# Output projection of the second attention: one fp32 product over 12 chunks, or three fp32r products key head by key head

## What is computed

```python
def _L1_xattn_ref(latents, context, Wq, Wk, Wv, Wo):
    H, KV, HD = (16, 4, 96)
    G = H // KV
    hidden = jnp.concatenate([context, latents], axis=1)
    q = (latents @ Wq.T).reshape(b, q_len, H, HD)
    k = (hidden @ Wk.T).reshape(b, s_len, KV, HD)
    v = (hidden @ Wv.T).reshape(b, s_len, KV, HD)
    ...
    scores = jnp.einsum('bkgqd,bksd->bkgqs', q, k) * scale
    attn = jax.nn.softmax(scores.astype(jnp.float32), axis=-1).astype(q.dtype)
    out = jnp.einsum('bkgqs,bksd->bkgqd', attn, v)
    return out.transpose(...).reshape(b, q_len, H * HD) @ Wo.T
...
x = x + jnp.tanh(g_xattn[1]) * _L1_xattn_ref(_layernorm(x), ctx_4096, ...)
```

## Time and profile before

| | us |
|---|---|
| median of 3 runs | 1620.5 (1618.6 to 1621.03) |
| the profiled execution, its time | 1619.05 |
| the profiled execution, first to last instruction (span) | 1617.3 |
| PE busy in it | 1572.8 (97%) |
| second attention, four pairs | 896.6 to 1257.5 |

### The profile page before, as it was taken

The page is one execution under the profiler, slowest core; times in us unless marked ns, Lnnn a source line. Parts: engine busy times, 40 slices in busy tenths (PEclk is TensorE's granted clock), DMA queues, the critical chain, the costliest instruction groups (busy, mean ns, idle before and its releaser), DMA issues.

```text
span 1617.3 us, 25912 instructions
## 1 busy us (share of the span) xinstructions
PE 1572.8 (97%) x8958; PEld 1264.1 (78%) x8958; DVE 981.2 (61%) x2633; ACT 742.1 (46%) x2151; POOL 399.3 (25%) x278
## 2 busy tenths in 40 slices
PE   8999999999999999999989999999999999899997
PEld 7888888888888888888875877868696788666556
DVE  6762663626636356363676774848576767756677
ACT  5442443424434244343433462735355332288873
POOL 3131320313203132032204300000001343376651
PEclk9999999999999999999999999999999999999999
DMA  5111111101111011110224000000001613000001
GB/s 179 54 43 34 59 45 41 42 29 55 42 52 42 29 55 42 52 43 30 79 79 195 14 1 14 0 13 0 0 1 41 223 52 107 14 14 14 1 1 53
DMA packets 34436, 76.22 MB, mean 47 GB/s; under 512 B 5569, under 2 KB 18497, under 8 KB 32193
## 3 DMA queue, kind: packets, MB, share of 16 engines
q1 hardware_dynamic: 34368, 75.36, 14.1%
HBM read 73.25 MB, written 2.10 MB: 47 GB/s over the span
## 4 chain that ended last, share of the span: by engine, by line
PE 78%; DVE 10%; ACT 5%; issue 3%; DVEq 2%; POOL 1%; DMA 1%; POOLq 0%; SPq 0%; ACTq 0%
PE banks L1183 11%; PE banks L1128 10%; PE banks L1101 9%; PE banks L1109 9%; PE banks L1333 9%; PE banks L1437 5%; PE banks L1239 4%; PE banks L1222 3%; PE banks L1409 3%; ACT p L978 2%; PE banks L1229 2%; PE banks L1540 2%; PE banks L1563 1%; PE banks L1357 1%; PE banks L1547 1%
## 5 line engine op out<-in xcount | busy, mean ns | idle before, releaser
L1183 PE MATMUL banks<-w_o,atT 128*128 128x512 f32 x720 | 180.2, 396 | 0.0
L527 POOL TENSOR_TENSOR w_q<-w_raw_q,w_q 128x1792 fp32r<-128x1792 f32 x15 | 61.1, 4070 | 479.6 <-ACT w_q L733 479.6
L1101 PE MATMUL banks<-cT,w_k 128*128 128x512 f32 x720 | 178.0, 396 | 0.0
L1128 PE MATMUL banks<-w_v,cT 128*128 128x512 f32 x768 | 176.6, 390 | 0.0
L1128 PEld LDWEIGHTS banks<-w_v,cT 128*128 128x128 f32 x768 | 143.9, 188 | 29.9
L1109 PE MATMUL banks<-xT,w_q 128*128 128x512 f32 x672 | 163.8, 394 | 0.7 <-ACT kT L723 0.7
L1874 DVE TENSOR_TENSOR sA<-banks,pbias 128x512 f32<-128x512 f32 x64 | 44.1, 690 | 186.5 <-PE banks L1222 185.8
L1183 PEld LDWEIGHTS banks<-w_o,atT 128*128 128x128 f32 x720 | 131.9, 188 | 25.7
L1101 PEld LDWEIGHTS banks<-cT,w_k 128*128 128x128 f32 x720 | 131.9, 188 | 25.6
L1109 PEld LDWEIGHTS banks<-xT,w_q 128*128 128x128 f32 x672 | 123.7, 188 | 26.1 <-ACT kT L723 1.1
L792 ACT ACTIVATE sA<-sA,nmA 128x128 f32<-128x128 f32 x256 | 99.5, 393 | 56.9 <-DVE nmA L1879 56.6
(11 more groups left out here) (280 smaller groups left out, 3273.7 us busy)
## 6 DMA issues: line engine op xcount, KB each, us to landing
w_raw_v<-in_w0v SPq DMA_DIRECT2D x8, 1024.0 KB, 4.8
w_raw_q<-in_w0q SPq DMA_DIRECT2D x16, 512.0 KB, 3.3
w_raw_k<-in_w0k SPq DMA_DIRECT2D x15, 512.0 KB, 3.5
w_raw_o<-in_w0o SPq DMA_DIRECT2D x15, 512.0 KB, 3.3
cTp<-in_ctxT SPq DMA_DIRECT2D x12, 512.0 KB, 4.0
wq_raw<-in_wq SPq DMA_DIRECT2D x1, 3072.0 KB, 10.4
wo<-in_wo SPq DMA_DIRECT2D x1, 3072.0 KB, 20.1
x_res<-in_x SPq DMA_DIRECT2D x4, 512.0 KB, 11.3
```

What stands on the lines that cost most here:

```text
L527: pool.tensor_tensor(w_part[slot][1][:], w_raw[slot][:], w_part[slot][0][:].bitcast(F32), ALU.subtract).then_inc(S(f"w{slot}_lo"), 1)
L1101: mm = pe.matmul(dst, wk_[l][:, c, h * P:(h + 1) * P], cT[r][:, c, half * HT:(half + 1) * HT], start=c == 0 and n == 0, stop=c == DC - 1 a ...
L1128: mm = pe.matmul(dst, cT[l][:, c, b * P:(b + 1) * P], wv_[r][:, c, :], start=n == 0, stop=n == 3 * DC - 1)
L1183: mm = pe.matmul(dst, atT[l][:, h, t], w[r][:, h, :], start=n == 0, stop=n == 5)
```

## The change

`at1` is now three tiles of one key head: `at1_raw` in fp32, written by ACT alone, and two fp32r parts, which DVE makes by a cast and a subtraction (both from SBUF to SBUF). The weight comes in quarters, one for each key head and pair (16 loads of 768 KB where there was one of 3 MB), into two slots used in turn; ACT rounds a quarter in three pieces of 128x512 (`out_high`) and POOL subtracts in three (`out_rest`). `project(kv, b)` is 9 fp32r matmuls, run one key head later, and DVE adds each result to x (`add_out`, eight additions for a pair where there were two). Bank 6 + b now alternates between queries and projection, which `added` and the order of the queries guard. The next pair's rows are normalised before the loop over key heads and turned inside the last one, in banks 6 and 7; in the last pair they are turned between the last two projections. The waits for `at1` ahead of the scores become waits for ACT's copy (`x1_ah`).

```diff
@@ -271,9 +268,18 @@
...
-        wo1 = sb(ctx_1, "wo1", [P, NCH * KV1, D])
+
+        wo1, wo1_raw = [], []
+        for k in range(2):
+            high_1 = sb(ctx_1, f"wo1_0_{k}", [P, NCH, D], F32R)
+            ctx_x = ExitStack()
+            wo1_raw.append(sb(ctx_x, f"wo1_raw_{k}", [P, NCH, D]))
+            ctx_x.close()
+            wo1.append([high_1, sb(ctx_1, f"wo1_1_{k}", [P, NCH, D], F32R)])
...
+        at1_raw = sb(ctx_1, "at1_raw", [P, NCH, PT2])
+        at1 = [sb(ctx_1, f"at1_{l}", [P, NCH, PT2], F32R) for l in range(2)]
...
@@ -459,14 +465,30 @@
...
-            sp.dma_start(wo1[:], A["wo1"]).then_inc(S("wo1_ld"), 16)
...
+                sp.dma_start(wo1_raw[kv % 2][:], A["wo1"][:, NCH * kv:NCH * (kv + 1), :]).then_inc(S("wo1_ld"), 16)
...
+            def next_out_weights(i, kvs):
+                for kv in range(kvs):
+                    sp.wait_ge(S("x1_out"), 8 * i + 2 * kv + 2)
+                    out_weights(KV1 * i + kv + 2, (kv + 2) % KV1)
...
@@ -609,8 +631,16 @@
...
+            def out_rest(i, kv):
+                for c in range(NCH):
+                    pool.wait_ge(S("w1_hi"), KV1 + NCH * (KV1 * i + kv) + c + 1)
+                    pool.tensor_tensor(wo1[kv % 2][1][:, c, :], wo1_raw[kv % 2][:, c, :],
+                                       wo1[kv % 2][0][:, c, :].bitcast(F32), ALU.subtract).then_inc(S("w1_lo"), 1)
...
+                for kv in range(KV1):
+                    out_rest(i, kv)
...
@@ -909,31 +939,54 @@
...
+                def out_high(kv, c0, c1):
+                    if c0 == 0:
+                        act.wait_ge(S("wo1_ld"), 16 * (KV1 * i + kv + 1))
+                    for c in range(c0, c1):
+                        act.activation(wo1[kv % 2][0][:, c, :], wo1_raw[kv % 2][:, c, :], ACT.Copy)\
+                           .then_inc(S("w1_hi"), 1)
...
-                def attended(kv, b):
-                    act.wait_ge(S("x1_pv"), 8 * i + 2 * kv + b + 1)
+                out_high(0, 0, NCH)
+
+                def attended(kv, b, heads=True, rest=True):
...
+                    if heads:
+                        act.wait_ge(S("x1_pv"), 8 * i + 2 * kv + b + 1)
+                        act.activation(at1_raw[0:HD1, :, t], src[0:HD1, 0:NCH], ACT.Copy)
+                    if rest:
...
+                            e = act.activation(at1_raw[HD1:P, c, t], src[c * BLK:(c + 1) * BLK, G1 - 1], ACT.Copy)
+                        e.then_inc(S("x1_ah"), 1)
 
                 for kv in range(KV1):
+                    more = kv + 1 < KV1
+                    if kv > 0:
+                        out_high(kv, 0, 1)
                     probs(kv, 0)
+                    if kv > 0 and more:
+                        out_high(kv, 1, NCH)
                     probs(kv, 1)
-                    for b in range(2):
-                        probsT(kv, b)
-                        if kv + 1 < KV1:
-                            queries(kv + 1, 2 * b, min(2 * b + 2, NCH))
-                        attended(kv, b)
+                    probsT(kv, 0)
+                    if more:
+                        queries(kv + 1, 0, 2)
+                    else:
+                        out_high(kv, 1, NCH)
+                    attended(kv, 0, rest=False)
+                    probsT(kv, 1)
+                    attended(kv, 0, heads=False)
+                    if more:
+                        queries(kv + 1, 2, NCH)
+                    elif not last:
+                        store_xnT(L1X, i + 1, (0, 1), (6, 7))
+                    attended(kv, 1)
                 if not last:
                     context_high(i + 1)
                 else:
                     act.wait_ge(S("ffn_ld"), 128)
                     high(f1p[0], ffn["f1"]["base"][:], "wf")
-                store_next(L1X, i, last)
+                    store_next(L1X, i, last)
...
@@ -1405,6 +1458,8 @@
...
+                        if h == 0 and kv > 0:
+                            pe.wait_ge(S("x1_ah"), 8 * i + 2 * kv + b - 1)
...
@@ -1432,43 +1487,62 @@
...
+                def project(kv, b):
+                    pe.wait_ge(S("x1_at"), 8 * i + 2 * kv + b + 1)
+                    pe.wait_ge(S("w1_lo"), KV1 + NCH * (KV1 * i + kv + 1))
+                    if kv + 1 == KV1:
+                        if last:
+                            pe.wait_ge(S("x1_added"), 6 * i + 2 * kv + b - 1)
+                        else:
+                            wait_parts(L1X, i + 1, b)
+                    for c in range(NCH):
+                        for n, (l, r) in enumerate(PASSES):
+                            mm = pe.matmul(bank(6 + b), at1[l][:, c, b * P:(b + 1) * P], wo1[kv % 2][r][:, c, :],
+                                           start=c == 0 and n == 0, stop=c == NCH - 1 and n == len(PASSES) - 1)
+                    mm.then_inc(S("x1_out"), 1)
+
+                def added(kv, b):
+                    pe.wait_ge(S("x1_added"), 6 * i + 2 * kv + b + 1)
 
                 for kv in range(KV1):
+                    more = kv + 1 < KV1
                     for b in range(2):
                         if kv == 0:
                             pe.wait_ge(S("v1_ready"), 4 * i + 3 + b)
-                        else:
-                            pe.wait_ge(S(f"x1_at{b}"), 4 * i + kv)
                         scores(kv, b)
-                    more = kv + 1 < KV1
-                    if more:
-                        pe.wait_ge(S("wq1_lo"), kv + 2)
+                        if 0 < kv and more:
+                            project(kv - 1, b)
+                    if kv == 0:
+                        pe.wait_ge(S("w1_lo"), kv + 2)
                         queries(kv + 1, 0, 2)
                         queries(kv + 1, 2, NCH, 0, 1)
-                    else:
-                        pe.wait_ge(S("wo1_ld"), 16)
-                        project(0, 0, 2 * NCH - 1)
+                    if not more:
+                        project(kv - 1, 0)
                     for b in range(2):
                         turn(kv, b)
-                        if more:
+                        if kv == 0:
                             queries(kv + 1, 2, NCH, b + 1, 2 * b + 2)
-                        else:
-                            project(0, 2 * (NCH + b) - 1, 2 * (NCH + b) + 1)
+                        elif more:
+                            if b == 0:
+                                pe.wait_ge(S("w1_lo"), kv + 2)
+                                added(kv - 1, 0)
+                                queries(kv + 1, 0, 1)
+                                queries(kv + 1, 1, 2, 0, 2)
+                            else:
+                                queries(kv + 1, 1, 2, 2, DC)
+                                added(kv - 1, 1)
+                                queries(kv + 1, 2, NCH)
+                        elif b == 0:
+                            project(kv - 1, 1)
+                        elif not last:
+                            for j in range(2):
+                                added(kv - 1, j)
+                                turn_half(L1X, i + 1, j, 6 + j)
                         attend(kv, b)
-                project(0, 2 * NCH + 3, NCH * (KV1 - 1))
-                pe.wait_ge(S("x1_at0"), 4 * i + 4)
-                project(0, NCH * (KV1 - 1), NCH * KV1)
-                project(1, 0, 2 * NCH - 1)
-                turn_next(L1X, i, last)
-                project(1, 2 * NCH - 1, NCH * (KV1 - 1))
-                pe.wait_ge(S("x1_at1"), 4 * i + 4)
-                project(1, NCH * (KV1 - 1), NCH * KV1)
+                project(KV1 - 1, 0)
+                if last:
+                    turn_next(L1X, i, last)
+                project(KV1 - 1, 1)
...
@@ -2107,32 +2181,58 @@
...
+                def attended(kv, b):
+                    t = slice(b * P, (b + 1) * P)
+                    dve.wait_ge(S("x1_ah"), 8 * i + 2 * kv + b + 1)
+                    dve.tensor_copy(at1[0][:, :, t], at1_raw[:, :, t])
+                    dve.drain()
+                    dve.tensor_tensor(at1[1][:, :, t], at1_raw[:, :, t], at1[0][:, :, t].bitcast(F32),
+                                      ALU.subtract).then_inc(S("x1_at"), 1)
...
+                def add_out(kv, b):
+                    dve.wait_ge(S("x1_out"), 8 * i + 2 * kv + b + 1)
...
+                                             in1=x_res[:, 2 * i + b, :], op0=ALU.mult, op1=ALU.add)\
+                       .then_inc(S("res" if kv + 1 == KV1 else "x1_added"), 1)
+
+                next_apply(L1X, i)
                 for kv in range(KV1):
+                    more = kv + 1 < KV1
                     row_max(kv, 0)
-                    row_max(kv, 1)
-                    norm(kv, 0)
-                    norm(kv, 1)
+                    if kv > 0:
+                        attended(kv - 1, 1)
+                    if kv == 0:
+                        row_max(kv, 1)
+                        norm(kv, 0)
+                        norm(kv, 1)
+                    elif more:
+                        add_out(kv - 1, 0)
+                        norm(kv, 0)
```

(31 more changed lines are left out.)

53 lines of the change are left out of this document (22 added, 31 removed).

## The result

| | before | after |
|---|---|---|
| median, us | 1620.23 (4 runs, 1618.6 to 1621.03) | **1649.22** (4 runs, 1644.92 to 1650.57) |
| ratio | | 1.018, 95% interval 1.0165 to 1.0194 |
| span of the profiled execution | 1617.3 | 1647.3 |

The page's line of busy time answers to the earlier trace rows. PE's busy time is only 3.2 us less, since the length of a matmul in it is modelled and grows with a lower clock or a late neighbour; what a matmul costs is read from the spacing of starts. PE's share falls from 97% to 95% because the span is longer.

The account below looks back on a forecast made before the run. PE, busy 97%, bounds the kernel. A pair: +14.0 middle heads, −8.7 last head, −0.2 first, so +5.1; four pairs 20.4 plus end 2.9 give +23.3 on 1619.05, 1642.4; median 1.45 above, stated as 1643, range 1624 to 1652.

Parts of the forecast that it names:

- case A: The forecast itself: all the costed waits appear, 1636 to 1652 us; chance 0.58.
- below 3.8: Sign of being wrong: PE's waits in a second-attention pair grow by less than 3.8 us.
- Projection, −15.4: 72 fp32r matmuls a pair at 0.233 replace 24 fp32 chunks at 0.859: 3.8 us less a pair, 15.4 in all.
- Middle heads, 20.2: Key heads 1 and 2 take 20.2 us instead of 13.2: 4.2 of projection, 2.8 of waits; +14.0 a pair.
- The hold: POOL's weight subtractions hold DVE's scaling of p in middle heads; first turn waits from 7.7 to 8.5 us.
- case B: POOL's pieces miss the scaling of p, about 2 us less a head: 1627 us; chance 0.24.
- Last key head, 20.0: Each pair's last head, with two projections and waits of 2.0 and 1.3, takes 20.0 us, not 28.7: −8.7.
- First head, −0.2: First key head and before: a 0.5 us wait goes, normalising moved to DVE gives 0.35 back; −0.2 a pair.
- Stage end, +2.9: Once, after the last pair: PE waits 2.7 us for POOL's f1base split, plus 0.2 more in this pair.
- Costed at nothing: SP's 16 weight loads of 768 KB arrive in time, so no ACT rounding waits; zero cost.
- C: Projections fill PE under the score-to-turn chain, waits stay as before, only matmuls change: 1605 us; chance 0.07.
- Rival E: POOL holds more than the scaling, the casts and subtractions too: over 1652 us; chance 0.06.

Follow-up runs that it names:

- end_fp32r: Kernel before, own order, each fp32 projection matmul replaced by three fp32r ones on rounded operands, low parts left out: 1604.2 us.
- q_early: Changed kernel, with only TensorE finishing chunk 1 of the next queries ahead of the middle heads' second turn: 1626.9 us.
- late_pieces: Changed kernel, with the rounding of weight chunks 1 and 2 of the middle heads moved behind the first pT copies: 1632.6 us.
- small_pieces: Changed kernel, with POOL's weight subtractions cut to 8 of 512 columns and the third pass reading rounded weights: 1630.8 us.
- best_a: late_q_early plus f1_wait, with both third-head projections ahead of the last head's first turn and the next rows' split earlier: 1607.5 us.
- f1_wait: Changed kernel, with TensorE's wait for POOL's split of f1base put behind the 16 f1ra matmuls of its first pair: 1645.9 us.
- fp32_by_head: Changed kernel's head-by-head order with the projection in fp32 on raw weights and rows, no weight rounding or POOL split: 1643.1 us.
- late_q_early: late_pieces, with TensorE also finishing chunk 1 of the next queries ahead of the second turn: 1615.9 us.

## Why the prediction was right, and where it was off

The forecast was 1643, the likeliest case A, range 1624 to 1652; measured 1649.2. (1642.4 and 1.45 make 1643.9, not 1643.) PE's named waits grew by 7.2 us a pair, and the prediction counted itself wrong below 3.8. Point by point:

- *Projection, −15.4.* Right: end_fp32r measured −15.0. The trace's own 0.859 and 0.233 decided it. By the four passes of a true fp32 product in the Trainium skill, FP8 and Floating Point Precision, section TensorE Precision Notes, the estimate was −20.6; the run doesn't bear it out.
- *Middle heads, 20.2.* Measured 21.1 and 20.5 (second pair, from first score to first score), 0.6 more on the mean. The waits are the three that were named, in the order in which they were named: turn behind the held scaling (0.91 against 0.8), first attention step (0.34 against 0.5), second behind ACT's order (1.02 against 1.15). The sum of 2.8 a head was short. Head 2 follows the walk (turn at 8.53 for 8.5, end at 20.48 for 20.2). In head 1 the first projection starts 2.46 us after the first score and not 1.9, behind a wait of 0.40 for the queries' lo part and one of 0.20 for that of `at1`; the addition to x waits for it, DVE begins to scale p at 5.85 and not 5.1, and the turn comes at 9.17. Taken out by q_early and late_pieces, the last two groups and the hold were worth 4.1 (20.48 to 16.40).
- *The hold.* Right in kind and size: case B put its absence at 1627; small_pieces, without it, came to 1630.8 and late_pieces to 1632.6. A held scaling went to 1.45 us, more than the 1.10 of the earlier trace rows. The ends that were read as 1351.5 and 1352.7 are 1351.58 and 1352.82 by these rows: a held scaling ends a little behind the piece, not with it (see the last section).
- *Last key head, 20.0.* Measured 20.07 in the second pair (1070.48 to 1090.55), with the waits of 1.85 and 1.02 for which the walk had 2.0 and 1.3.
- *First head, −0.2.* In the second pair the part ahead of head 1 took 34.0 for 34.8: −0.8.
- *Stage end, +2.9.* The wait was 2.85 for 2.7. Counted from the last head's first score, PE was free at 22.1 for 20.2 and POOL's split ended at 24.7 for 22.8, both late alike, of which 1.6 us are PE's lower clock. Neither that nor the low clock behind the wait was in the sum.
- *Costed at nothing.* Right for the 16 loads: they landed in 4.4 us (median), and ACT's rounding waited for none.

So the term that was too small is the middle heads' +14.0, which measured +15.1 in the second pair. With −8.6 for the last head and −0.8 ahead of them it makes +5.7; that the first part gave 0.8 and not 0.2 hid half of the miss, which is luck. The pair's +5.1 measured +5.6 and +5.7 in the two inner pairs and +6.1 in the first. The two spans differ by 30.0 us, and the sum had 23.3. The pairs' excess over 5.1 makes 0.5 to 1.0 each, some 2.7 us in all (for the last pair an estimate: its +10.3 without the 2.9 of the end and the 1.6 of the clock). The other 4 us are the lower clock, for which the sum had nothing: in three places (below) it makes the changed kernel fall behind by 1.3, 1.6 and 1.7 us, and in the later stages it gets 1.1 back.

Of the rivals, C (1605, the chain stays covered) was wrong for this change and right about what can be had: best_a reached 1607.5 with the same arithmetic. What decided was where ACT's and POOL's work, one query chunk and the third head's second projection stood. Rival E's cast is held (0.84 us at most, 0.43 as a rule, the view of its line in the changed kernel). The hold of the cast costs little: with it, in late_pieces, the last heads' turns wait 7.3 us in all, and without it, in small_pieces, 5.5.

```profile
L2187 DVE CAST at<-at_raw x32: 424/426/840, 934.4 to 1279.5; 128x384 fp32r<-128x384 f32 x32
L2189 DVE TENSOR_TENSOR at<-at_raw,at x32: 557/558/559, 934.9 to 1280.0; 128x384 fp32r<-128x384 f32 x32
```

The subtraction's 558 ns never change, but none of its 32 instances overlaps a piece of POOL, in this kernel or in the other eight that have it. The Trainium skill, SBUF — State Buffer, section Who interferes with whom, lets it be held too, as it has two operands in SBUF. Another stage of the same trace agrees: an instruction of the same kind, 128x512 with both operands in SBUF, takes 1144 ns where it meets POOL (whose instruction runs from 1373.88 to 1374.62), and 676 to 679 the other three times.

```profile
L2509 DVE TENSOR_TENSOR zp<-zp,sc x4: 676/678/1144, 1374.0 to 1376.3; 128x512 f32<-128x512 f32 x4
```

So what kept the new subtraction free was its place and not its kind.

## What to carry to other kernels

Before splitting an operand on POOL, walk its pieces against VectorE's instructions from SBUF to SBUF, by the longest instance in a line's view and not by the median; then place the pieces where VectorE reads from PSUM. A copy that itself waits for TensorE should not stand ahead of one that TensorE waits for; here it was better to finish its source earlier (22.3 us) than to reorder the copies (8.2). A late operand can cost more than the wait that the profile names, because the operands derived from it come late in turn: in the one head that was taken apart, 2.75 us for 1.36.

## What the runs showed of the hardware

**TensorE's clock after waits.** In the changed kernel the windows view, for the stretch around the last pair's first turn (which waited 1.87 us) and for the `f1ra` matmuls behind the wait of 2.85, grants less than the full clock; before, this place had 1.00.

```profile
1269.00:1275.00 6.00, 5.92 (x23) 0.72 0.45 186
...
1288.00:1291.00 3.00, 3.00 (x14) 0.54 1.03 412
```

This is the lower of the two levels (1.2 GHz) for part of each stretch: 16 `f1ra` matmuls took 3.2 us and not 1.8, and nine of the projection 3.7 and not 2.1 (1269.92 to 1273.63). Waits as long (1.85 in the second pair) had no such effect, so it is not a certain price; f1_wait, without the wait, kept the full clock there. Shorter waits can have it: in fp32_by_head the clock fell behind the wait of 1.02 at the second attention step of head 2, in all four pairs. The kernel before, whose waits in this stage are 0.6 us at most, and late_q_early and best_a show no fall in the stage. One more such stretch, at 41 us, fell into the changed kernel and not into the one before, behind a wait of 2.16 us that both have (16 matmuls took 2.92 us from start to start, 1.78 before). It made up most of the 1.6 us by which the stage began late (898.24 for 896.62). It is no effect of the change: late_pieces and late_q_early have it too, and the other kernels with the change don't. So the clock differs between executions of like programs; of the four runs of the changed kernel the fastest (1644.92) has a mean granted clock of 0.998, the others 0.993 to 0.995.

**Who is held by POOL, and until when.** While POOL subtracts in SBUF, VectorE's scaling (SBUF to SBUF, 0.35 us) takes up to 1.45 and its cast (0.43) up to 0.84, in q_early 1.01; the subtraction of pT, with one operand in PSUM, takes 0.68 all the same. A held instruction ends at a fixed distance behind the end of the piece: the 16 held scalings of 128x256 in the changed kernel 0.15 us behind it, the 8 casts of 128x384 that take 0.82 or more 0.28. Here is one of them, POOL and then DVE: the piece ends at 1053.54, the cast at 1053.82.

```profile
1052.25 1.29 POOL L637 TENSOR_TENSOR wo<-wo_raw,wo 128x512 fp32r<-128x512 f32 x1 [14.66 <-ACT wo L946]
```

```profile
1052.99 0.83 DVE L2187 CAST at<-at_raw 128x384 fp32r<-128x384 f32 x1
```

So the hold can be computed from where the piece ends and the VectorE instruction starts. And where two pieces stand back to back, the second goes ahead of the next scaling: in the head shown above the second scaling ends 0.15 behind the first piece (1036.30), the third 0.15 behind the second piece (1037.59), and only the fourth is free again (0.34 us).
